# Moving the two quantisation activations of a tile ahead of two weight-sum steps in the first stage of an attention and FFN kernel

## What is computed

```
xn  = (x - mean) / sqrt(var + 1e-5)                    # per row
att = softmax(q k' / 8) v, 16 heads, then the output projection with wo
xq  = round(xn * 127 / max|xn|) * max|xn| / 127        # per row, 8-bit grid
wq  = clip(round(w / mean|w|), -1, 1) * mean|w|        # w1 (4096 x 1024) and w2 (1024 x 4096)
ffn = bit_linear(silu(depthwise_conv3(bit_linear(xn, w1))), w2)
out = x + att + ffn
```

## Time and profile before

| | |
|---|---|
| profiled execution, device time | 2134.6 us |
| span of the slowest core (core 1) | 2133.0 us |
| spans of cores 0 to 7 | 2132.4, 2133.0, 2117.6, 2127.7, 2130.3, 2130.9, 2127.4, 2119.2 us |
| granted TensorE clock, die 0 and die 1 | 0.896, 0.894 |
| PE busy | 1446.3 us (68%) |
| ACT busy | 1163.8 us (55%) |
| DVE busy | 923.5 us (43%) |
| `wf<-w_t` loads over the whole kernel | 128, 512 KB each, 4.0 us to landing |

### The profile page before, as it was taken

One profiled execution on the slowest core, in us unless ns is written; L12 is line 12 of the kernel. 1 busy time (PEld: TensorE's weight loads), 2 busy tenths in 40 slices (PEclk: granted clock), 3 DMA queues, 4 the chain that ended last, 5 costly groups with the idle time before them and its releaser, 6 DMA issues.

```text
span 2133.0 us, 24777 instructions; the slowest of 8 cores (2117.6 to 2133.0 us)
## 1 busy us (share of the span) xinstructions
PE 1446.3 (68%) x6986; PEld 540.8 (25%) x6986; DVE 923.5 (43%) x1328; ACT 1163.8 (55%) x1395; POOL 101.3 (5%) x193
## 2 busy tenths in 40 slices
PE   0111588888888889887774986566675676566755
PEld 0111232222222222222111333232222222222222
DVE  4566213333334333333221237678317741785143
ACT  4666038888788888878871013276105620563044
POOL 0000000000000000000000001111001100110000
PEclk9999969999899999989776998888987888888878
DMA  6665303222322222212103012222352234223445
GB/s 181 201 203 200 87 17 78 65 67 68 71 69 74 65 70 65 72 52 70 59 30 59 1 35 75 79 70 65 94 138 65 66 105 136 79 70 97 140 117 140
DMA packets 117956, 186.35 MB, mean 87 GB/s; under 512 B 44482, under 2 KB 77379, under 8 KB 117828
## 3 DMA queue, kind: packets, MB, share of 16 engines
q10 hardware_dynamic: 36864, 83.90, 12.9%
q0 software_dynamic: 16864, 50.35, 9.6%
q1 hardware_dynamic: 64100, 50.52, 8.1%
HBM read 167.95 MB, written 25.17 MB: 91 GB/s over the span
## 4 chain that ended last, share of the span: by engine, by line
PE 47%; DVE 15%; DMA 14%; ACT 12%; issue 11%; ACTq 1%; DVEq 1%; SPq 0%; POOL 0%; POOLq 0%
DMA wf<-w_t 6%; PE psC L553 6%; PE psA L882 6%; ACT probs L625 6%; PE psA L588 5%; PE psC L929 5%; PE psD L517 5%; DVE amax L1054 4%; PE psC L557 4%; DMA w2q_sb<-w2q_stage 3%; PE psA L740 3%; PE psD L529 2%; DVE u_sb L1073 2%; DVE denrow L701 2%; ACT wf L206 2%
## 5 line engine op out<-in xcount | busy, mean ns | idle before, releaser
L625 ACT ACTIVATE probs<-psA,bias_exp 128x1024 bf16<-128x1024 f32 x512 | 549.7, 1109 | 100.0 <-PE psA L591 99.1
L882 PE MATMUL psA<-xqT,w1q_sb 128*128 128x512 bf16 x1024 | 291.4, 435 | 159.4 <-DVE u_sb L1078 95.5
L553 PE MATMUL psC<-probs,vroll 128*65 128x512 bf16 x512 | 207.2, 405 | 138.5 <-ACT probs L625 83.5
L792 ACT ACTIVATE u_sb<-psA,cws 128x512 f32<-128x512 f32 x128 | 87.1, 681 | 271.4 <-PE psA L887 271.0
L929 PE MATMUL psC<-w2q_sb,hq 128*128 128x512 bf16 x576 | 169.0, 405 | 74.4 <-DMA w2q_sb<-w2q_stage 44.5
L814 ACT ACTIVATE qscr<-qscr,meff 128x512 f32<-128x512 f32 x128 | 91.5, 715 | 225.4 <-DVE qscr L1089 212.3
L591 PE MATMUL psA<-qroll,kroll 64*128 64x512 bf16 x512 | 208.0, 406 | 0.0
L588 PE MATMUL psA<-qroll,kroll 64*128 64x512 bf16 x512 | 208.0, 406 | 0.0
L557 PE MATMUL psC<-probs,vroll 128*65 128x512 bf16 x512 | 204.7, 400 | 0.0
L882 PEld LDWEIGHTS psA<-xqT,w1q_sb 128*128 128x128 bf16 x1024 | 100.7, 107 | 288.0 <-issue 218.9
L517 PE MATMUL psD<-xnT,wblk 128*128 128x512 bf16 x512 | 139.5, 400 | 10.3 <-DVE qroll L669 4.5
(11 more groups left out here) (139 smaller groups left out, 1864.1 us busy)
## 6 DMA issues: line engine op xcount, KB each, us to landing
wf<-w_t ACTq DMA_DIRECT2D x128, 512.0 KB, 4.0
w1q_sb<-w1q_stage POOLq DMA_DIRECT2D x128, 256.0 KB, 2.9
w2q_sb<-w2q_stage SPq DMA_DIRECT2D x128, 128.0 KB, 2.3
w2q_sb<-w2q_stage ACTq DMA_DIRECT2D x128, 128.0 KB, 2.2
x_t<-x SPq DMA_DIRECT2D x16, 512.0 KB, 5.5
w1q_stage<-wqb SPq DMA_DIRECT2D x32, 256.0 KB, 2.6
w2q_stage<-wqb SPq DMA_DIRECT2D x32, 256.0 KB, 2.0
xr_t<-x POOLq DMA_DIRECT2D x32, 256.0 KB, 4.2
```

The lines of the kernel that those rows point to most:

```text
L553: t.matmul(psC[0:65, 0:512], v_v[:, qvj % 2, kcj, laj, 0:65], probs[:, pslot * 1024:pslot * 1024 + 512], start=(kcj == 0), stop=(kcj == NT ...
L625: s.activation(out=probs[:, pslot * 1024:(pslot + 1) * 1024], in_=psA[:, pp * 1024:(pp + 1) * 1024], func=AF.Exp, scale=0.125, bias=bias_e ...
L882: t.matmul(ps[:, 0:512], w1q_sb[:, b * 1024 + cc * 128:b * 1024 + (cc + 1) * 128], xqTv[:, cc, tb * 512:tb * 512 + 512], start=(cc == 0), ...
```

## The change

In the loop over tiles on ACT, the call of `quant_tail(i - 1)` moves from between chunks b and c to ahead of chunk a. Nothing is added or removed, and no semaphore or buffer changes.

```
             inc("p1sqrt")
+            if i >= 1:
+                quant_tail(i - 1)
             for ch in (4 * i, 4 * i + 1):
                 wabs(ch)
                 if ch + 2 < NW:
                     wdma(ch + 2)
-            if i >= 1:
-                quant_tail(i - 1)
             for ch in (4 * i + 2, 4 * i + 3):
                 wabs(ch)
                 if ch + 2 < NW:
                     wdma(ch + 2)
```

## The result

The changed kernel takes 2164.61 us, the median of 12 runs (2158.28 to 2199.98), against 2136.67 us for the kernel before (31 runs). The ratio is 1.0124, with a 95% interval of 1.0104 to 1.0143: 26 us slower. The two medians lie 27.9 us apart, because each holds one slow run (2199.98 and 2173.21 us) that the ratio leaves out. The forecast was 2155 us, with a range of 2141 to 2171. The profiled execution's slowest core is core 4 here and was core 1 before, so wherever single cores could mislead I give means over the eight cores.

The account below looks back on a forecast made before the run. ACT's chain of waits for chunk loads was taken to bound the first stage; 18.1 us on 14 tiles plus 2.1 at the stage's end, 20.2 us over 2134.6, gave 2155 us, range 2141 to 2171.

Parts of the forecast that it names:

- What bounds the stage, and the direction: First stage: ACT's waits for chunk loads set it; they grow about 18 us, from 43.8, and the kernel gets slower.
- The pair runs early without a wait, a and b gain little: ACT, tile loop: pair's input ready 5.9 us before its new place; a and b wait only for the hand-over.
- The tile is 9.1 + L, with L the larger landing: First-stage tile: 9.1 us plus L, the larger issue-to-landing time of c and d; longer than now above L = 3.7.
- L = 5.0: Landing of c and d, 5.0 us (3.9 to 6.0): tile 14.1 us, 1.29 more, 18.1 us over 14 tiles.
- the first rival: Chunks c and d, issued later, meet less traffic: L 4.2 us, tile 13.3 us, time 2144 us; chance 17%.
- The end of the stage, 2.1 us: Tile 15: PE's last transposes start 2.1 us later, held by ACT, and POOL's first projection load moves equally.
- The shift of what follows: After the first stage: no instruction moved, booked as a plain shift at nothing; a few us either way possible.
- The sum: Whole kernel: 18.1 us on tiles plus 2.1 at the stage's end, 20.2 us over 2134.6, forecast 2155 us.
- Prefetch wins: First stage: a and b always ready, c and d land fastest; L 3.2 us, 2130 us, not slower; chance 6%.
- The jam: x_t and c loads collide as x_t and d did: L 6.5, tile 15.6 us, time 2176 us; chance 13%.
- the 20% given for no visible change: Whole kernel: chance of a time within about 0.5% (10.7 us) of before, 2124 to 2146 us.
- the slower case: Whole kernel: time above the 2124 to 2146 us band of no visible change; chance 77%.

Follow-up runs that it names:

- Experiments 1 and 2: Three chunk loads in flight instead of two; 1: on the kernel before, ratio 0.9913; 2: on the changed kernel, 0.9978; both ratios against the kernel before.
- Experiments 3 and 6: Changed kernel; 3: x_t loads cut to 128 of 1024 columns, ratio 1.0085; 6: x_t load held until Abs of c, 1.0055; both against the kernel before.
- experiment 8: Changed kernel with each chunk load from chunk 3 on cut to 512 of 1024 columns: ratio 1.0015 against the kernel before.

## Why the prediction was right, and where its size was off

*What bounds the stage, and the direction.* Right. ACT's wait for `wf` is what grew (34.5 us more where I had written 18), ACT's and DVE's work did not. Experiments 1 and 2 show it from the other side: one more load ahead takes away most of the loss together with the wait, 2.01 us a tile down to 0.70.

*The pair runs early without a wait, a and b gain little.* Right, as the timeline shows. Tile 8 hid a part: over all 112 tiles ACT's idle time before the Abs of a and b was 0.11 and 0.84 us before, and is 0.00 and 0.51 us now. Some 0.44 us a tile was gained there, which the forecast's sum contains, since it builds the new tile from its start.

*The tile is 9.1 + L, with L the larger landing.* Right in form, in every tile. The constant is 8.93 in tile 8, since the pair behind the short root takes 2.33 us in place of 2.50, and 8.98 in the mean of all tiles.

*L = 5.0.* This is the mis-sized term. It measured 14.73 - 8.98 = 5.75 us, and 14 x 0.75 = 10.5 us are missing from the forecast for it. The forecast had averaged two landings of d with the median of all chunk loads, 4.6 us. That median is pulled down by the loads of a, b and c (4.4 us each in the median, core 1). The d loads alone, in the kernel before, had a median of 5.7 us on core 1. And the forecast had called L the larger of two landings but sized it as a single one. In the changed kernel c and d take 5.53 and 5.50 us in the mean of all cores, and the larger of the two in each tile 5.75: so about 0.5 us of the miss is the single landing, and 0.25 the larger of two. Experiments 3 and 6 show what in it is x_t: 0.8 to 0.9 us. The idea behind the first rival, that c and d would meet less traffic behind x_t, was wrong. From before to after, in the mean of all cores, d's landing hardly changed (5.61 to 5.50 us) and c's grew from 4.33 to 5.53 us. It was x_t's own load that landed sooner (first fence: before, from 27.2 us; second: after, core 4; the 13 loads of tiles 3 to 15).

```profile
DMA to landing us min/median/max: 4.3/5.1/7.2
```

```profile
DMA to landing us min/median/max: 3.2/3.9/4.8
```

*The end of the stage, 2.1 us.* 2.2 on the profiled cores, 1.6 in the mean. ACT's L221 holds PE's last transposes, as forecast. Tile 15 starts at 236.19 us and POOL's load at 253.24 on core 4, where 225 and 241.6 had been written, because of L.

*The shift of what follows.* Booked at nothing, came out at -4.3 us in the profiled execution, within the scatter allowed for.

*The sum.* 20.2 us forecast, 26.8 in the profiled execution (mean of the cores): 10.5 too little on L, 1.7 too much through the constant (14 x 0.12), 1.3 too little because the mean core's tile was 12.72 and not 12.81 us, 0.5 too much at the end of the stage, 1.4 of later start not foreseen, and 4.3 given back behind the stage (0.1 is rounding). The last I read as scatter; it happened to bring the sum nearer to the forecast. The Trainium skill's figure for a transfer (page "DMA: Bandwidth & Descriptors", section "Anatomy of one DMA — SWDGE (gpsimd) path"), an estimate of 3.2 us for 512 KB, fits the fastest loads here as before (3.1 us), and no typical one; the measurement decides.

*The rivals.* Prefetch wins: no, every one of c's 14 landings on core 4 was 4.1 us or more. The jam: partly, single c loads reached 6.8 us, but the tile never went to 15.6 in the mean of any core (14.87 at most). The later issues meeting less traffic: no, L was 5.75 us and not 4.2.

*The chances.* They don't add up as written: the first rival (17%), the prefetch case nearly whole (6%) and a little of the forecast come to more than the 20% given for no visible change, and with 3% for faster the slower case is left with less than 77%.

## What to carry to other kernels

A load that an engine issues itself, in line with its arithmetic, is hidden by exactly the work that stands between the issue and the need; so work that covers nothing else should be spread between the loads. Standing together it covered a and b, which needed little more, and left c and d exposed. Before pricing such a move, take the landing of the very load that will be exposed, tile by tile the larger one where two are, and the place at which it is issued now in the median tile, waits included. And where a free buffer exists, one more load ahead is worth more than the best order: 1.3 us a tile here in the old order, 2.6 in the new.

## What the runs showed of the hardware

All eight cores were loading in every run, so how much of a landing comes from the other cores' traffic is not shown.

A 512 KB chunk load landed in 3.1 us at best. With hardly any x_t traffic, c and d, issued 1.66 us apart, took 4.2 and 4.8 us (experiment 3), and 5.9 and 5.8 us with the whole x_t load 1.1 us ahead of c (the changed kernel; medians of the slowest cores). At 256 KB a and b took 3.0 us and c and d 4.0 (experiment 8).

Of x_t and c, issued 1.1 us apart in the changed kernel, the first was the fast one: 3.8 and 5.7 us in the mean of all cores. I had expected the stagger to help the second too. In the kernel before, 32 pairs of x_t and d were issued 1.0 to 1.4 us apart, and there both took about the same, 5.2 and 5.4 us; the load of c had gone out ahead of x_t's in that kernel. So the distance alone does not say which is fast, and no run here separates it from what else is in flight. Issued within 0.5 us of one another, x_t and d took 6.1 and 6.3 us in the mean of 30 pairs; the 7.2 and 7.0 us of the earlier trace rows are among the longest of them.
